# Both normalisations on ScalarE instead of VectorE, with a new order of the work on every engine

## What is computed

```
n1     = (x - mean(x)) * rsqrt(var(x) + 1e-5) * g1 + b1
q,k,v  = n1 @ wq + bq, n1 @ wk + bk, n1 @ wv + bv      (split in 8 heads)
scores = q k^T / sqrt(32) + (0.1 * adj * adj where adj > 0, else -inf)
x1     = x + (softmax(scores) v) @ wo + bo
n2     = (x1 - mean(x1)) * rsqrt(var(x1) + 1e-5) * g2 + b2
out    = x1 + gelu(n2 @ w1 + bias1) @ w2 + bias2
```

## Time and profile before

| | before |
|---|---|
| median of 3 runs | 1495.12 us (1494.67 to 1496.03) |
| the profiled execution, its own time | 1498.11 us |
| its span, first to last instruction | 1496.3 us |
| TensorE matmul busy | 1382.7 us (92%) |
| VectorE busy | 1296.4 us (87%) |
| ScalarE busy | 1026.7 us (69%) |
| GpSimd busy | 529.1 us (35%) |
| mean granted TensorE clock | 0.98 |

### The profile page before, as it was taken

How to read it: one execution, slowest core, us unless ns; L and a number is a source line. 1 busy time by engine, 2 the same in 40 slices (tenths; PEclk the granted TensorE clock), 3 DMA queues, 4 the chain that set the end, 5 groups by cost and what they waited for, 6 DMA issues and landing times.

```text
span 1496.3 us, 33799 instructions
## 1 busy us (share of the span) xinstructions
PE 1382.7 (92%) x11580; PEld 1168.6 (78%) x11580; DVE 1296.4 (87%) x2258; ACT 1026.7 (69%) x3080; POOL 529.1 (35%) x424
## 2 busy tenths in 40 slices
PE   7689999999999999999999999999999999999988
PEld 6567788778788778788778788777778877878867
DVE  4888989899989899898999898999898999898863
ACT  3666777767777766778766677766677776677752
POOL 2344322444332444332344432344432244432210
PEclk9789999999999999999999999999999999999989
DMA  4443334443334343333344333344433444332330
GB/s 141 134 134 121 113 100 132 128 147 119 122 104 127 120 144 129 123 104 121 116 144 133 124 111 108 124 136 139 127 112 98 130 130 147 119 112 99 110 108 25
DMA packets 147255, 180.14 MB, mean 120 GB/s; under 512 B 13584, under 2 KB 130576, under 8 KB 147216
## 3 DMA queue, kind: packets, MB, share of 16 engines
q1 hardware_dynamic: 147216, 179.63, 37.7%
HBM read 95.69 MB, written 83.89 MB: 120 GB/s over the span
## 4 chain that ended last, share of the span: by engine, by line
PE 54%; DVE 16%; ACT 12%; issue 12%; POOL 5%; DVEq 0%; DMA 0%; ACTq 0%; POOLq 0%; SPq 0%
PE work L369 17%; PE work L370 14%; PE work L371 14%; ACT soft L603 6%; DVE wa_raw L816 5%; POOL rstd L1009 4%; PE work L445 4%; DVE soft L804 3%; ACT L603 3%; DVE soft L780 2%; PE work L471 2%; PE area L425 2%; ACT late_memory L661 2%; ACT qk_all L646 1%; DVE x L837 1%
## 5 line engine op out<-in xcount | busy, mean ns | idle before, releaser
L603 ACT ACTIVATE soft<-soft,nmax 128x128 f32<-128x128 f32 x1024 | 396.8, 393 | 102.8 <-DVE nmax L788 102.3
L1006 POOL TENSOR_TENSOR ve<-mv,eps 128x4 f32<-128x4 f32 x64 | 13.8, 216 | 890.8 <-DVE mv L853 812.7
L369 PE MATMUL work<-w_hi,hid_parts 128*128 128x256 f32 x1024 | 289.5, 283 | 0.6 <-DVE res L920 0.6
L371 PE MATMUL work<-w_hi,hid_parts 128*128 128x256 f32 x1024 | 286.6, 280 | 0.0
L370 PE MATMUL work<-w_lo,hid_parts 128*128 128x256 f32 x1024 | 285.8, 279 | 0.0
L646 ACT ACTIVATE qk_all<-work,bqk_col 128x512 f32<-128x512 f32 x128 | 87.7, 687 | 194.5 <-PE work L371 194.5
L909 DVE TENSOR_TENSOR hid_parts<-late_memory,hid_parts 128x512 fp32r<-128x512 f32 x256 | 172.3, 683 | 55.2 <-ACT hid_parts L671 55.2
L369 PE MATMUL work<-nt_hi,w_hi 128*128 128x512 f32 x512 | 209.0, 408 | 1.9 <-DVE nt_lo L899 1.9
L661 ACT ACTIVATE late_memory<-work,b_col 128x512 f32<-128x512 f32 x256 | 174.5, 683 | 52.4 <-PE work L371 50.2
L370 PE MATMUL work<-nt_lo,w_hi 128*128 128x512 f32 x512 | 202.3, 395 | 0.0
L371 PE MATMUL work<-nt_hi,w_lo 128*128 128x512 f32 x512 | 200.7, 392 | 0.0
(11 more groups left out here) (90 smaller groups left out, 3053.6 us busy)
## 6 DMA issues: line engine op xcount, KB each, us to landing
moved_blocks<-wa_raw SPq DMA_DIRECT2D x128, 512.0 KB, 2.6
probt<-moved_blocks SPq DMA_DIRECT2D x512, 128.0 KB, 2.8
xin<-in_x SPq DMA_DIRECT2D x32, 512.0 KB, 4.5
out<-res SPq DMA_DIRECT2D x128, 128.0 KB, 2.3
adj_in<-in_adj SPq DMA_DIRECT2D x32, 256.0 KB, 3.3
res<-in_L_gnn_w SPq DMA_DIRECT2D x1, 1024.0 KB, 10.5
late_memory<-in_L_gnn_w SPq DMA_DIRECT2D x1, 1024.0 KB, 12.2
wa_raw<-in_L_gnn_wq SPq DMA_DIRECT2D x1, 256.0 KB, 3.9
```

What stands on the lines that cost most here:

```text
L369: pe.matmul(o, lhs_hi, rhs_hi, start=first, stop=False)
L371: return pe.matmul(o, lhs_lo, rhs_hi, start=False, stop=last)
L603: a = act.activation(soft[:, b % 2, h, :], soft[:, b % 2, h, :], ACT.Exp, bias=nmax[:, b % 2, h:h + 1], accum_out=rsum[:, b % 2, h:h + 1])
```

## The change

- `norm1` and `norm2` become ScalarE activations (`Identity`) with a scale and a bias for each partition: `rstd * x + shift`, with `shift = (0 - mean) * rstd`. VectorE loses both.
- GpSimd's `rstd` makes the shift: two more instructions of 128x4 each time, one before the power and one that waits for it.
- The order of all bodies and the table `UNITS` are new. On TensorE, `mix` of sequence 0 moves from the end of a step to the start of the next one, `query_key` 2 and 3 as well, while `values` 0 moves to the end of the step before.
- In the first group, `setup` on VectorE (low parts of three weights) comes right after the first statistics.

In the diff, "..." in the three long bodies stands where the old order was; it is in the kernel above.

```diff
@@ -42,12 +42,12 @@
 LAND = RPB * 16
-UNITS = [("v", 0, 0, 0), ("nt", 0, -2, 1), ("nt", 1, -2, 2), ("proj", 0, -1, 3), ("v", 1, 0, 0),
-         ("mix", 1, -1, 3), ("up", 0, -2, 1), ("up", 1, -2, 2), ("up", 2, -2, 0), ("up", 3, -2, 1),
-         ("proj", 1, -1, 3), ("up", 4, -2, 2), ("up", 5, -2, 0), ("mix", 2, -1, 3), ("up", 6, -2, 1),
-         ("up", 7, -2, 2), ("proj", 2, -1, 3), ("down", 0, -2, 0), ("xt", 0, 1, 1), ("xt", 1, 1, 2),
-         ("mix", 3, -1, 3), ("down", 1, -2, 0), ("proj", 3, -1, 3), ("down", 2, -2, 1), ("down", 3, -2, 2),
-         ("qk", 0, 1, 0), ("qk", 1, 1, 1), ("qk", 2, 1, 2), ("mix", 0, 0, 3), ("qk", 3, 1, 0)]
+UNITS = [("mix", 0, -1, 3), ("nt", 0, -2, 0), ("nt", 1, -2, 1), ("qk", 2, 0, 2), ("qk", 3, 0, 0),
+         ("up", 0, -2, 1), ("proj", 0, -1, 3), ("up", 1, -2, 2), ("v", 1, 0, 0), ("up", 2, -2, 1),
+         ("mix", 1, -1, 3), ("up", 3, -2, 2), ("up", 4, -2, 0), ("proj", 1, -1, 3), ("up", 5, -2, 1),
+         ("up", 6, -2, 2), ("mix", 2, -1, 3), ("up", 7, -2, 0), ("proj", 2, -1, 3), ("xt", 0, 1, 1),
+         ("xt", 1, 1, 2), ("down", 0, -2, 0), ("mix", 3, -1, 3), ("down", 1, -2, 1), ("down", 2, -2, 2),
+         ("proj", 3, -1, 3), ("qk", 0, 1, 0), ("down", 3, -2, 1), ("v", 0, 1, 2), ("qk", 1, 1, 0)]
 PLACE = {(kind, i): at for at, (kind, i, _, _) in enumerate(UNITS)}
 PER_GROUP = {"down": GB, "v": 2, "qk": 4, "up": FC, "xt": DC, "nt": DC, "mix": GB, "proj": GB}
 FIRST, EARLY, LATE = -2, 4, 2
@@ -177,6 +177,11 @@
+        less1 = sb("less1", [P, GB])
+        less2 = sb("less2", [P, GB])
+        shift1 = sb("shift1", [P, GB])
+        shift2 = sb("shift2", [P, GB])
+        zeros = sb("zeros", [P, GB])
@@ -226,11 +231,13 @@
+        x_powered = sem("x_powered")
+        n_powered = sem("n_powered")
@@ -325,6 +332,7 @@
 sp.dma_start(w2_raw, w2.rearrange(chunked, p=P)).then_inc(w2_loaded, 16)
 def body(step):
+    fetch_blocks(step, -1, 1)
     send_blocks(step, -1, 2)
     load_adj(step, 2)
     fetch_blocks(step, -1, 2)
@@ -332,13 +340,12 @@
     fetch_blocks(step, -1, 3)
     store(step, -2, 0)
     send_blocks(step, 0, 0)
+    store(step, -2, 1)
     fetch_blocks(step, 0, 0)
-    store(step, -2, 1)
+    store(step, -2, 2)
     send_blocks(step, 0, 1)
-    store(step, -2, 2)
+    store(step, -2, 3)
     load_x(step, 2)
-    store(step, -2, 3)
-    fetch_blocks(step, 0, 1)
 steps(sp, groups, body)
@@ -535,40 +542,40 @@
     mm.then_inc(full["down"], 1)
 def body(step):
...
+    mix(step, -1, 0)
     flip(step, -2, "nt", 0)
     flip(step, -2, "nt", 1)
+    query_key(step, 0, 2)
+    query_key(step, 0, 3)
+    up(step, -2, 0)
+    project_out(step, -1, 0)
+    up(step, -2, 1)
+    values(step, 0, 1)
     score(step, 0, 0)
...
+    up(step, -2, 2)
     mix(step, -1, 1)
...
     up(step, -2, 3)
+    up(step, -2, 4)
     project_out(step, -1, 1)
...
     up(step, -2, 5)
+    up(step, -2, 6)
     mix(step, -1, 2)
...
+    score(step, 0, 1)
     up(step, -2, 7)
...
     project_out(step, -1, 2)
...
     flip(step, 1, "xt", 0)
     flip(step, 1, "xt", 1)
+    down(step, -2, 0)
+    score(step, 0, 2)
     mix(step, -1, 3)
...
     down(step, -2, 1)
+    down(step, -2, 2)
     project_out(step, -1, 3)
...
+    query_key(step, 1, 0)
+    score(step, 0, 3)
     down(step, -2, 3)
...
+    values(step, 1, 0)
     query_key(step, 1, 1)
...
 steps(pe, groups, body)
@@ -650,6 +657,26 @@
         act.wait_ge(wa_loaded[3], 16)
         act.activation(wa_hi[:, 3, :, :], wa_raw[:, 3, :, :], ACT.Copy).then_inc(hi_made, 1)
+def norm1(step, off, b):
+    if not step.has(off):
+        return
+    if b == 0:
+        act.wait_ge(x_rstd, step.through(off, 1, 0))
+        need(act, full["xt"], step.through(off - 1, DC, DC - 1))
+    act.activation(xhat[:, b, :], xin[:, step.parity_of(off), b, :], ACT.Identity,
+                   scale=rstd1[:, b:b + 1], bias=shift1[:, b:b + 1]).then_inc(xhat_ready, 1)
+def norm2(step, off, b):
+    if not step.has(off):
+        return
+    if b == 0:
+        act.wait_ge(n_rstd, step.through(off, 1, 0))
+        need(act, full["nt"], step.through(off - 1, DC, DC - 1))
+        if step.at_first(off):
+            act.wait_ge(lo_made, 7)
+    act.activation(nhat[:, b, :], x1[:, step.parity_of(off), b, :], ACT.Identity,
+                   scale=rstd2[:, b:b + 1], bias=shift2[:, b:b + 1]).then_inc(nhat_ready, 1)
 def gelu(step, off, m):
     if not step.has(off):
         return
@@ -671,44 +698,52 @@
     act.activation(hid_hi[:, m, :], hid[:, m % 3, :], ACT.Copy).then_inc(hid_hi_ready, 1)
 def body(step):
...
+    query_key_copy(step, 0, 1)
+    attn_hi(step, -1, 0)
     flip_hi(step, -2, "nt", 0)
     flip_hi(step, -2, "nt", 1)
     exponential(step, -1, 3, 1)
...
+    query_key_copy(step, 0, 2)
+    exponential(step, -1, 3, 0)
+    query_key_copy(step, 0, 3)
     gelu(step, -2, 0)
     hidden_hi(step, -2, 0)
     gelu(step, -2, 1)
     hidden_hi(step, -2, 1)
+    values_copy(step, 0, 1)
     gelu(step, -2, 2)
+    attn_hi(step, -1, 1)
+    norm1(step, 1, 0)
+    norm1(step, 1, 1)
     gelu(step, -2, 3)
+    norm1(step, 1, 2)
+    gelu(step, -2, 4)
     hidden_hi(step, -2, 2)
...
+    norm1(step, 1, 3)
     hidden_hi(step, -2, 3)
     hidden_hi(step, -2, 4)
     gelu(step, -2, 5)
+    gelu(step, -2, 6)
     attn_hi(step, -1, 2)
     hidden_hi(step, -2, 5)
...
     hidden_hi(step, -2, 6)
     gelu(step, -2, 7)
     hidden_hi(step, -2, 7)
+    flip_hi(step, 1, "xt", 0)
     exponential(step, 0, 0, 1)
+    flip_hi(step, 1, "xt", 1)
     exponential(step, 0, 0, 0)
...
     attn_hi(step, -1, 3)
     exponential(step, 0, 1, 0)
     exponential(step, 0, 1, 1)
+    query_key_copy(step, 1, 0)
     exponential(step, 0, 2, 1)
     exponential(step, 0, 2, 0)
...
+    norm2(step, -1, 0)
+    norm2(step, -1, 1)
+    norm2(step, -1, 2)
+    norm2(step, -1, 3)
+    values_copy(step, 1, 0)
     if not step.steady and step.n == 0:
         late_hi()
@@ -867,28 +902,8 @@
     for b in range(GB):
         a = dve.bn_aggr(mv1[:, b, :], st1[:, b, :])
     a.then_inc(x_stats, 1)
...
-def norm1(step, off, b):
...
-        dve.wait_ge(x_rstd, step.through(off, 1, 0))
-        need(dve, full["xt"], step.through(off - 1, DC, DC - 1))
-    dve.tensor_scalar(xhat[:, b, :], xin[:, par, b, :], mv1[:, b, 0:1], rstd1[:, b:b + 1],
-                      ALU.subtract, ALU.mult).then_inc(xhat_ready, 1)
-    if step.at_first(off) and b == GB - 1:
+    if step.at_first(off):
         setup()
...
-def norm2(step, off, b):
...
-        dve.wait_ge(n_rstd, step.through(off, 1, 0))
-        need(dve, full["nt"], step.through(off - 1, DC, DC - 1))
-    dve.tensor_scalar(nhat[:, b, :], x1[:, par, b, :], mv2[:, b, 0:1], rstd2[:, b:b + 1],
-                      ALU.subtract, ALU.mult).then_inc(nhat_ready, 1)
 def flip_lo(step, off, kind, c):
     if not step.has(off):
@@ -921,64 +936,56 @@
                       res[:, par, b, :], ALU.add).then_inc(taken["down"], 1)
 def body(step):
+    flip_lo(step, -2, "nt", 0)
+    attn_lo(step, -1, 0)
+    invert(step, -1, 2)
+    flip_lo(step, -2, "nt", 1)
+    normalise(step, -1, 2)
+    turn_blocks(step, -1, 2)
+    invert(step, -1, 3)
+    normalise(step, -1, 3)
     stats1(step, 1)
     residual(step, -1, 0)
...
+    hidden_lo(step, -2, 0)
     add_edges(step, 0, 0)
+    attn_lo(step, -1, 1)
+    hidden_lo(step, -2, 1)
     turn_blocks(step, -1, 3)
...
     residual(step, -1, 1)
...
     hidden_lo(step, -2, 2)
     hidden_lo(step, -2, 3)
+    maximum(step, 0, 0)
     hidden_lo(step, -2, 4)
...
+    attn_lo(step, -1, 2)
     hidden_lo(step, -2, 5)
...
+    stats2_of(step, -1, 0)
     hidden_lo(step, -2, 6)
     add_edges(step, 0, 1)
     hidden_lo(step, -2, 7)
     residual(step, -1, 2)
+    maximum(step, 0, 1)
+    result(step, -2, 0)
+    flip_lo(step, 1, "xt", 0)
+    flip_lo(step, 1, "xt", 1)
     stats2_of(step, -1, 1)
...
     stats2_of(step, -1, 2)
...
     invert(step, 0, 0)
     normalise(step, 0, 0)
+    turn_blocks(step, 0, 0)
     attn_lo(step, -1, 3)
...
+    result(step, -2, 1)
     add_edges(step, 0, 2)
+    maximum(step, 0, 2)
     residual(step, -1, 3)
...
     stats2_of(step, -1, 3)
+    stats2(step, -1)
     invert(step, 0, 1)
...
+    result(step, -2, 2)
     normalise(step, 0, 1)
...
     turn_blocks(step, 0, 1)
...
+    result(step, -2, 3)
     add_edges(step, 0, 3)
...
     maximum(step, 0, 3)
...
     if not step.steady and step.n == 0:
         late_lo()
@@ -996,23 +1003,29 @@
                    base=0, pattern=[[-1, P]], channel_multiplier=1).then_inc(ident_ready, 1)
 pool.memset(mhalf[:, :], -0.5).then_inc(mhalf_set, 1)
 pool.memset(eps[:, :], EPS).then_inc(mhalf_set, 1)
-pool.wait_ge(mhalf_set, 2)
-def rstd(step, off, stats, mv, ve, veps, o, done):
+pool.memset(zeros[:, :], 0.0).then_inc(mhalf_set, 1)
+pool.wait_ge(mhalf_set, 3)
+def rstd(step, off, stats, mv, ve, veps, o, powered, less, shift, done):
     if not step.has(off):
         return
     pool.wait_ge(stats, step.through(off, 1, 0))
```

(52 more changed lines are left out.)

51 lines of the change are left out of this document (removed).

## The result

The changed kernel takes 1407.93 us (median of 4 runs, 1407.62 to 1414.14) against 1494.89 us in the same comparison: ratio 0.943, 95% interval 0.9402 to 0.9458. It is faster by 87 us.

What follows compares the result with a forecast made beforehand. TensorE was taken as nearest its limit, with two waits a step. Steps of 42.3 for 44.58 us, 29 times, save 66; end saves 3, start loses 2: 1495.1 - 67 = 1428 us, range 1410 to 1462.

Steps and rivals of the forecast that it cites:

- the first hole: TensorE's idle 1.73 us in each step before VectorE's `result` frees a bank, blamed on `norm2` in VectorE's queue.
- the wait of 0.91 us for the power: VectorE's normalisation waits 0.91 us for GpSimd's power, named as part of the queue that delays `result`.
- rival C: Slower: Identity between Gelus on ScalarE forces table loads of 1.283 us, a step 48.7 us, about 1610 us; chance 0.04.
- The walk: TensorE's unit starts in the new order set against each release: one unavoidable wait of 0.35 us, a step of 42.2.
- slack "nearly zero" at down1: TensorE's `down` 1, at 27.4 us, needs VectorE's low part of xt0, put at 27.35 us.
- rival A: Further waits in the new order from thin slacks: a step of 43.5 to 44.1 us, 1463 to 1480 us; chance 0.14.
- B: No net change: another wait takes all of the 2.75 us available in a step, 1492 to 1498 us; chance 0.03.
- D: Slower: ScalarE becomes the bound with activations of 1 us and more, over 45 us a step, 1510 us; chance 0.03.
- TensorE's floor: A step without TensorE's two waits, 44.58 - 1.73 - 1.02 = 41.83 us, claimed because the matmuls stay the same.
- the two holes: TensorE's waits in a step: 1.73 us for VectorE's `result`, 1.02 us for ScalarE's copy of `query_key` 3.
- my sum: Whole run: 29 steps gain 2.28 us each, 66; the end gains 3, the start loses 2; together -67 us.
- Rival E: Better: the wait before nt0 disappears or the end gains more, 41.85 us a step, 1411 us; no separate chance.

Runs made afterwards that it cites:

- act_norms_old_order: Kernel before with only the two normalisations and GpSimd's shift moved to ScalarE, all other orders as before: 1430.3 us, ratio 0.956.
- gpsimd_order_2: Kernel before with one GpSimd line moved, `residual_start` ahead of the second rstd, normalisations still on VectorE: 1432.8 us, ratio 0.958.
- flip_then_score: Changed kernel with `score` 2 on TensorE right behind the transposes of xt, ahead of `down` 0: 1443.0 us, ratio 0.965 to the kernel before.
- norm2_twice: Changed kernel with each `norm2` issued a second time on ScalarE, into a tile nobody reads: 1473.2 us in one run.
- banks_swapped: Changed kernel with other PSUM banks for the transposes of nt and the units up to `up` 5: 1397.3 us, ratio 0.934 to the kernel before.

## Why the prediction was right or wrong

**What bounds the kernel.** Right, and shown twice: the first hole came from `norm2` meeting GpSimd's `residual_start`. Moving the normalisations away (act_norms_old_order) and moving only GpSimd's instruction (gpsimd_order_2) both give 42.67 us. What I also blamed, the wait of 0.91 us for the power, is still there in gpsimd_order_2 and costs nothing.

**The costs of the parts.** Right: 0.59 us for an activation was forecast, 0.591 and 0.596 measured; no table load was added, so rival C falls. Here the trace agrees with what I had cited of the Trainium skill, ScalarE: Activation LUTs, Table sets: the hidden batching unit: Identity between two Gelus needs no load. GpSimd's two small instructions cost no time in a steady step (the one wait of 9.2 us for the shift is in the last group, ScalarE having nothing else to do). VectorE's busy time fell by 3.3 us a step, not by 6.5: 1.8 us of the difference are the clash, which moved on to `hidden_lo` (5.4 to 7.2 us a step). A part of the rest is that instructions overlap a little, so that taking eight away takes less busy time off than the sum of their durations. I had also cited the Trainium skill, Perfetto Trace Analysis, Optimizing Scalar/DVE Operations, for moving work when VectorE is saturated; by gpsimd_order_2 it was not saturation that cost time here.

**The walk.** It held nearly everywhere. Counted from the end of `query_key` 1 (759.64): nt0 starts 1.01 us later (1.02 forecast), 0.34 us of it as a wait (0.35); `norm2` begins 2.64 us ahead (2.6), and ScalarE is idle for 0.27 us before the copy (0.2). The slack "nearly zero" at down1 was none to play with, as flip_then_score shows. So rival A, further waits, did not come, nor B or D. norm2_twice shows that D's mechanism is real: 2 us more on ScalarE at that place are 1.6 us more in a step.

**The step that failed: TensorE's floor.** I wrote "Without the two a step is 44.58 - 1.73 - 1.02 = 41.83 us. That is TensorE's floor, since the change gives it the same matmuls". It measured 41.29 (banks_swapped). The same matmuls do not take the same time in another order. About 0.28 us are what the restart behind the two holes costs beyond the wait, and I had its start in my own rows: behind 803.49 the next matmul follows after 0.34, not 0.23 us. At the first hole it comes to 0.18 us, measured, since closing 1.73 us took 1.91 off the step; at the second it is 0.10 us by the issue distances. The other 0.26 us are neighbours: the transposes are followed by narrow matmuls before and by wide ones after, which takes about 0.3 us off them. This second part is read from issue distances and was not tried by itself; the total is measured. With 41.29 + 0.35 the same working gives 41.64, which is the measured step. Over the 29 steps of my sum the floor is 15.7 us of the 23 that were missing, and the 0.1 us a step that I added for small misses is 3 more.

**Start and end.** The 27 steps gave 79.2 us, the rest of the run 11.0, where my sum had 4.6 for two more steps, 3 for the end and 2 lost at the start, 5.6 in all. The waits at the end were sized nearly right. In the last step but one TensorE waits for 7.0 us in all before the change (5.9 of them for `nt`) and for 3.3 after it, most of them now for a low part:

```profile
1340.14 0.33 PE L478 MATMUL work<-ident,late_memory 128*128 128x128 f32 x1 [0.16 <-ACT late_memory L677]
1340.64 0.76 PE L478 MATMUL work<-ident,late_memory 128*128 128x128 f32 x5 [0.17 <-ACT late_memory L677]
1343.53 0.47 PE L376 MATMUL work<-nt_hi,w_hi 128*128 128x512 f32 x1 [2.12 <-DVE nt_lo L914]
```

That is 3.7 us against the 3 in my sum. What the sum did not have at all is TensorE's clock. The stretches ahead of the first power and behind the second, in the kernel before:

```profile
0.00:173.35 173.35, 139.70 (x1084) 118.19 (x1085) 137.15 (x249) 103.16 (x324) 56.58 (x56) 0.88 0.40 126
1377.12:1496.30 119.18, 104.10 (x779) 88.62 (x777) 71.81 (x120) 61.40 (x165) 25.53 (x17) 0.93 0.25 81
```

The same two in the changed kernel:

```profile
0.00:171.08 171.08, 137.76 (x1100) 116.97 (x1101) 128.72 (x222) 116.18 (x351) 60.91 (x72) 0.92 0.41 128
1295.64:1406.10 110.46, 99.59 (x762) 84.97 (x760) 64.78 (x107) 66.13 (x178) 26.98 (x22) 0.97 0.26 87
```

Behind the second power the clock is at its lower level for 17.4 us before and 6.8 after, with matmuls busy for 13.0 and 5.7 of them. At that level a matmul of 512 columns is issued every 0.43 us (1437.06 to 1437.49 in the kernel before) and not every 0.23, so that about half of the busy time is lost: some 3.6 us less after the change, an estimate. Waits over the whole stretch fall by 4.3 us (12.4 to 8.1), and the two make 7.9 of the 8.7. Ahead of the first power the lower level lasts 41.0 us before and 27.3 after, which by the same estimate gives 4 us and covers the 2.3 that the start gained in spite of its later first transpose. The one execution of the changed kernel that took 1414.14 us had a mean granted clock of 0.981, the others 0.984 to 0.988. No run holds the clock fixed, so this is read and not shown.

**The range.** Its lower end, 1410, allowed for no wait at all with a floor of 41.83. It had nothing for the floor itself being wrong, since I held it for measured. It was a difference of two measured things, not a measurement. Rival E, the better case, also had a slip: 79 us in the steps, 3 at the end and 2 lost at the start come to 1415 us, not 1411, so that the range had even less below the forecast than I believed.

**The change as a whole.** Of the 2.93 us of a step, 1.91 belong to the end of the clash, which one moved line on GpSimd also gives. The new order is worth 1.02 more (42.67 to 41.65), and in full only together with the move: with `norm2` on VectorE it gives 0.6 us at full clock where the clash is left (44.58 to 43.98), which the slower steps take back, and 0.2 where it is gone (42.67 to 42.47).

## What to carry to other kernels

When an instruction has two durations in a profile, look first at what runs on the other engine at that moment: moving one line on GpSimd did as much as moving the work to another engine. A floor got by taking waits off a step still holds the refills behind those waits and the neighbours of that order; read units of work in undisturbed places and sum these. Before a producer is moved back in one queue, follow the DMA queue that waits for it, and what stands behind in that queue. And before two step lengths are compared, look at the granted clock of each step: in four kernels here a part of the mean was the clock and not the order.
